# Spike encoding on Trainium2: x in four loads with a semaphore each, and the four lines of a step interleaved in memory

## The reference

```python
rates = relu(x) * 0.001
def step(voltage, rate_t):                 # 1024 steps; voltage starts at cond
    for _ in range(4):                     # four substeps
        voltage = voltage + rate_t
        spikes = floor(voltage)
        voltage = voltage - spikes
    return voltage, spikes                 # spikes of the last substep
h = all_spikes / 0.001
x = x + mixer(h, ...)                      # q, k, v projections, convolutions, delta rule, gates
x = x + experts(recurrence(cond, x), ...)  # gated recurrence, then top-1 of 8 experts
```

## Time and profile before

| | us |
|---|---|
| median of 3 runs | 1087.11 |
| lowest, highest | 1082.46, 1088.53 |
| profiled execution, its own time | 1088.54 |
| its span | 1086.6 |

### The profile page before, as it was taken

How to read it: one execution, slowest core, us unless ns; L and a number is a source line. 1 busy time by engine, 2 the same in 40 slices (tenths; PEclk the granted TensorE clock), 3 DMA queues, 4 the chain that set the end, 5 groups by cost and what they waited for, 6 DMA issues and landing times. The chain is left out here.

```text
span 1086.6 us, 13995 instructions
## 1 busy us (share of the span) xinstructions
PE 762.9 (70%) x5174; PEld 467.3 (43%) x5174; DVE 686.6 (63%) x967; ACT 496.0 (46%) x816; POOL 252.8 (23%) x227
## 2 busy tenths in 40 slices
PE   4720009979777055585865848999992779999995
PEld 1300003326657045574433414444441547667674
DVE  4999937872744999557579541999995413332331
ACT  5888735530433122365534414999993112222321
POOL 0000000000202000000050330799894023343331
PEclk9965559975778558898877869999996569999997
DMA  6700010000682000000200009100001911111100
GB/s 224 246 0 0 0 50 0 0 1 0 190 239 76 0 2 2 21 4 14 78 0 0 1 0 346 61 0 1 0 1 30 369 61 39 34 51 38 35 16 0
DMA packets 35509, 60.57 MB, mean 56 GB/s; under 512 B 8027, under 2 KB 22491, under 8 KB 34754
## 3 DMA queue, kind: packets, MB, share of 16 engines
q1 hardware_dynamic: 29826, 51.27, 14.6%
q0 software_dynamic: 3312, 6.31, 1.9%
q10 hardware_dynamic: 2304, 2.10, 0.6%
HBM read 55.20 MB, written 7.21 MB: 57 GB/s over the span
## 5 line engine op out<-in xcount | busy, mean ns | idle before, releaser
L1797 ACT ACTIVATE moe_ht<-x_tr,moe_b 128x128 f32<-128x128 f32 x184 | 49.9, 382 | 147.6 <-PE x_tr L1762 147.6
L1076 POOL TENSOR_TENSOR path<-path,mix_pr 128x1280 f32<-128x1280 f32 x16 | 38.3, 2424 | 247.7 <-DVE mix_pr L1238 247.7
L1753 PE MATMUL x_y<-moe_w,moe_ht 128*128 x368 | 85.0, 385 | 2.1 <-ACT moe_ht L1797 2.1
L1744 PE MATMUL x_hid<-w,moe_xt 128*128 x184 | 85.7, 610 | 0.9 <-DVE moe_xt L1887 0.7
L1753 PEld LDWEIGHTS x_y<-moe_w,moe_ht 128*128 128x128 f32 x368 | 69.4, 193 | 11.6 <-issue 2.8
L1894 DVE COPY moe_hid<-x_hid 128x512 f32<-128x512 f32 x46 | 31.9, 692 | 64.6 <-PE x_hid L1744 64.6
L205 PE MATMUL bad_sum<-spike_bad,ones 128*128 128x16 f32 x2 | 0.6, 386 | 88.5 <-ACT spike_outside L171 88.5
L1406 PE MATMUL r_bank<-recur_h_other,recur_wg 128*128 128x512 f32 x128 | 60.2, 592 | 0.0
L1402 PE MATMUL r_bank<-recur_zw,eye 128*128 128x512 f32 x112 | 57.2, 592 | 0.8 <-ACT recur_zw L1437 0.8
L201 PE MATMUL w_bank<-spike_wbuf,spike_pick 128*128 128x512 f32 x80 | 39.6, 655 | 21.2 <-DMA spike_wbuf<-in_gW 21.2
L367 PE MATMUL pj<-hs,proj_wqkv 128*128 128x512 f32 x96 | 46.4, 634 | 11.5 <-DMA mix_st<-in_c_spread 11.5
(11 more groups left out here) (274 smaller groups left out, 1878.2 us busy)
## 6 DMA issues: line engine op xcount, KB each, us to landing
spike_wbuf<-in_gW SPq DMA_DIRECT2D x8, 1280.0 KB, 6.2
w<-in_w1T SPq DMA_DIRECT2D x8, 1024.0 KB, 12.4
moe_w<-in_w2T SPq DMA_DIRECT2D x8, 1024.0 KB, 10.9
fir_band<-in_band_l SPq DMA_DIRECT2D x11, 512.0 KB
xT<-in_xT SPq DMA_DIRECT2D x4, 1024.0 KB, 6.0
fir_band<-in_band_m SPq DMA_DIRECT2D x11, 312.0 KB
mix_st<-in_band_l SPq DMA_DIRECT2D x5, 512.0 KB
z_rows<-recur_change SPq DMA_DIRECT2D x8, 256.0 KB, 3.8
```

The source lines that it names most:

```text
L1076: nc.gpsimd.tensor_tensor(x, x, w, ALU.mult).then_inc(s.weighted, 1)
L1744: last = nc.tensor.matmul(hid_bank[n][:], xt[:, c, :], m.w1[:, bass.ds(e, 1), c, n * N:(n + 1) * N].rearrange("p o n -> p (o n)"), start=( ...
L1753: last = nc.tensor.matmul(y_bank[:], ht[:, k, :], w2[:, bass.ds(e, 1), k, :].rearrange("p o n -> p (o n)"), start=(k == 0), stop=(k == K2 ...
L1797: nc.scalar.activation(ht[:, k, :], tr_bank[k // (K2 // 2)][:, k % (K2 // 2) * P:(k % (K2 // 2) + 1) * P], ACT.Relu, bias=b1[:, bass.ds(e, ...
```

## The change

Two edits in `load_and_spike`.

1. x comes in four loads of half a megabyte, one for each column group, each with a semaphore of its own. The two loads of the condition come first, with a semaphore `v_in`, and the pick matrix has `pick_in`. ScalarE's slope and VectorE's lines of the first four units wait for their own part; VectorE's first copy waits for the condition only, TensorE for the pick matrix. `done_with` has 27 semaphores instead of 22.
2. `line` is `[P, TU, SUB]`: the four substeps of a step lie side by side. First count reads it and writes `count` in order. The scan of L225 and the three L230 instructions now read and write `line` with a step of four float32 (16 bytes); they read their rates in order as before.

```diff
--- before.py
+++ after.py
@@ -68,7 +68,7 @@
         rate1 = [sb(f"rate1_{i}", [P, TU]) for i in range(2)]
         rate4 = [sb(f"rate4_{i}", [P, TU]) for i in range(2)]
         rate = [sb(f"rate{i}", [P, SU]) for i in range(RING)]
-        line = [sb(f"line{i}", [P, SUB, TU]) for i in range(2)]
+        line = [sb(f"line{i}", [P, TU, SUB]) for i in range(2)]
         volt = [sb(f"volt{i}", [P, SU]) for i in range(RING)]
         count = [sb(f"count{i}", [P, 2 + SU], I16) for i in range(RING)]
         over = [sb(f"over{i}", [P, 2 + SU], I16) for i in range(RING)]
@@ -88,14 +88,15 @@
         wbuf = sb("wbuf", [P, 2, W_CHUNK, HF])
         w_bank = own.enter_context(nc.psum_tensor("w_bank", [P, HF], F32))
         bad_sum = own.enter_context(nc.psum_tensor("bad_sum", [P, 2 * UNITS], F32))
-        (x_in, edge_set, w_used, started, rated, rated4, spread, summed, lined, rounded,
+        (v_in, pick_in, edge_set, w_used, started, rated, rated4, spread, summed, lined, rounded,
          counted, scanned2, flagged, recounted, corrected, scanned3, checked, spiked, joined,
          exact) = map(sem, (
-             "x_in", "edge_set", "w_used", "started", "rated", "rated4", "spread", "summed",
+             "v_in", "pick_in", "edge_set", "w_used", "started", "rated", "rated4", "spread", "summed",
              "lined", "rounded", "counted", "scanned2", "flagged", "recounted", "corrected", "scanned3", "checked",
              "spiked", "joined", "exact"))
         w_in = [sem(f"gate_w_in{i}") for i in range(2)]
-        m.done_with = [x_in, edge_set, w_used, started, rated, rated4, spread, summed, lined, rounded, counted, scanned2,
+        x_in = [sem(f"x_in{j}") for j in range(J)]
+        m.done_with = [*x_in, v_in, pick_in, edge_set, w_used, started, rated, rated4, spread, summed, lined, rounded, counted, scanned2,
                        flagged, recounted, corrected, scanned3, checked, spiked, joined, exact, *w_in]
 
         w_stat = d.gW1[D:, :].rearrange("(k p) n -> p k n", p=P)
@@ -106,9 +107,11 @@
         @block.sync
         def _(sp):
             for c in range(C):
-                sp.dma_start(m.xT[:, c * B:(c + 1) * B, :], d.xT[c * P:(c + 1) * P]).then_inc(x_in, 16)
-                sp.dma_start(v0[:, c * B:(c + 1) * B], d.condT[c * P:(c + 1) * P]).then_inc(x_in, 16)
-            sp.dma_start(pick[:], d.c_pick).then_inc(x_in, 16)
+                sp.dma_start(v0[:, c * B:(c + 1) * B], d.condT[c * P:(c + 1) * P]).then_inc(v_in, 16)
+            for j in range(J):
+                c, b = divmod(j, B)
+                sp.dma_start(m.xT[:, j, :], d.xT[c * P:(c + 1) * P, b]).then_inc(x_in[j], 16)
+            sp.dma_start(pick[:], d.c_pick).then_inc(pick_in, 16)
             for ch in range(CHUNKS):
                 if ch >= 2:
                     sp.wait_ge(w_used, ch - 1)
@@ -126,9 +129,10 @@
         @block.scalar
         def _(act):
             act.wait_ge(edge_set, 2 * RING + 3)
-            act.wait_ge(x_in, 5 * 16)
 
             def slope(u):
+                if u < J:
+                    act.wait_ge(x_in[u], 16)
                 if u >= 2:
                     act.wait_ge(summed, u - 1)
                 nc.scalar.activation(rate4[u % 2][:], x_of(u), ACT.Relu, scale=float(SUB * DT)).then_inc(rated4, 1)
@@ -146,7 +150,7 @@
                 act.wait_ge(lined, u + 1)
                 if u >= RING:
                     act.wait_ge(corrected, u - RING + 1)
-                nc.scalar.activation(count[i][:, 2:].rearrange("p (t s) -> p s t", s=SUB), line[u % 2][:], ACT.Relu,
+                nc.scalar.activation(count[i][:, 2:], line[u % 2][:].rearrange("p t s -> p (t s)"), ACT.Relu,
                                      bias=mid[:]).then_inc(rounded, 1)
 
             def flag(u):
@@ -191,7 +195,7 @@
 
         @block.tensor
         def _(pe):
-            pe.wait_ge(x_in, 5 * 16)
+            pe.wait_ge(pick_in, 16)
             for ch in range(CHUNKS):
                 pe.wait_ge(w_in[ch % 2], 16 * (ch // 2 + 1))
                 for i in range(W_CHUNK):
@@ -206,7 +210,7 @@
 
         @block.vector
         def _(dve):
-            dve.wait_ge(x_in, 5 * 16)
+            dve.wait_ge(v_in, C * 16)
             dve.wait_ge(edge_set, 2 * RING + 3)
             nc.vector.tensor_copy(v_start[:], v0[:]).then_inc(started, 1)
             dve.wait_ge(started, 1)
@@ -214,6 +218,8 @@
             def lines(u):
                 part, j = divmod(u, J)
                 i = u % 2
+                if u < J:
+                    dve.wait_ge(x_in[u], 16)
                 if u >= 2:
                     dve.wait_ge(spread, u - 1)
                 if part:
@@ -222,13 +228,13 @@
                 dve.wait_ge(rated4, u + 1)
                 if u >= 2:
                     dve.wait_ge(rounded, u - 1)
-                nc.vector.tensor_tensor_scan(line[i][:, SUB - 1, :], rate4[i][:], rate4[i][:], v_start[:, j:j + 1],
+                nc.vector.tensor_tensor_scan(line[i][:, :, SUB - 1], rate4[i][:], rate4[i][:], v_start[:, j:j + 1],
                                              ALU.add, ALU.bypass).then_inc(summed, 1)
                 dve.wait_ge(rated, u + 1)
                 dve.wait_ge(summed, u + 1)
                 for k in range(SUB - 1):
-                    last = nc.vector.scalar_tensor_tensor(line[i][:, k, :], rate1[i][:], float(k + 1 - SUB),
-                                                          line[i][:, SUB - 1, :], ALU.mult, ALU.add)
+                    last = nc.vector.scalar_tensor_tensor(line[i][:, :, k], rate1[i][:], float(k + 1 - SUB),
+                                                          line[i][:, :, SUB - 1], ALU.mult, ALU.add)
                 last.then_inc(lined, 1)
 
             def second_scan(u):
```

## The result

| | before | after |
|---|---|---|
| median of 19 runs each | 1085.47 us | 1090.85 us |
| lowest, highest | 1080.89, 1089.68 | 1085.54, 1093.46 |
| ratio, 95% interval | | 1.0049, 1.0033 to 1.0064 |
| span of the profiled execution | 1086.6 us | 1087.8 us |

The change makes the kernel 5.4 us slower. The forecast had the direction and about twice the size (+10.3 us).

A forecast was written before the change was run, and what follows sets the result against it. VectorE was taken to bound the spike stage. Start -4.3, first count -1.4, clears +0.3, lines +15.3, scans +0.4 summed to +10.3 us: 1097 us on a base of 1087.11, range 1083 to 1102.

The forecast's parts named there:

- VectorE sets the pace, and its gain or loss comes out one for one: Spike stage from 22.06 us to VectorE's last scan: VectorE alone sets the pace; its changes reach the stage's end fully.
- ScalarE's 23 us are worth only the first wait: First count in order: ScalarE 23 us less busy, but only VectorE's first wait for it counts, -1.4 us.
- Five clears, +0.3: SP clears five more semaphores ahead of the projection's loads, 0.06 us each: +0.3 us, all on the path.
- Part 0, -4.3: Start of the spike stage: first half megabyte of x lands at about 7.5 us instead of 11.75, -4.3 us.
- the late bound of 8.6: Part 0's landing in us if a half megabyte takes as long as the first whole megabyte (3.9 + 4.7).
- The lines, +15.3: 24 L230 instructions on VectorE, stepping 16 bytes, go from 688 to 1332 ns each: +15.3 us.
- I take the last: Price for VectorE's 16-byte step taken from ScalarE's L149, 2.29 ns an element, over VectorE's short and long rows.
- the middle rival: Lines priced by VectorE's long transpose rows: +8.2 us, sum +2.8, 1089.9 us; chance 0.27.
- The short rows: VectorE's short stepped instructions as price for the lines: 0.2 us as fixed cost, 4.0 us by the word.
- The scans, +0.4: Eight VectorE scans writing the line at a 16-byte step: +0.05 us each, +0.4 us in all.
- Read and write add up: Rival for the lines: a stepped read and a stepped write on VectorE add their costs, +25 us, 1112; chance 0.06.
- The page's 2.50: Skill page's ns a column for a destination stepping 24 words; L230 would grow 0.75 us, the sum be 14.

The follow-up runs named there:

- e7_x_first: Changed kernel with lines as two interleaved pairs, and part 0 of x issued ahead of the condition's two loads; one run, 1078.4 us.
- the probe: Kernel before plus a block ahead of the spike stage measuring VectorE and ScalarE instructions at various steps; run once for its trace, no kernel time given.

## Why the prediction was wrong

- **VectorE sets the pace, and its gain or loss comes out one for one**: right up to the stage's end, where -3.45 - 1.44 + 9.7 = +4.8 stand against +4.7 measured at the cast. With the 0.3 and 0.4 us behind it, and 0.2 more until the loads have landed, that is +5.6 at the first matmul, and +5.4 in the median.
- **ScalarE's 23 us are worth only the first wait**: right. 8 x 2.9 us went, 1.44 us of it counted, and its idle time ahead of the check grew.
- **Five clears, +0.3**: right, 0.28. Another 0.37 us at the barrier were not foreseen.
- **Part 0, -4.3**: -3.45. The landing was put at 7.5 and came at 8.4, near the late bound of 8.6. The terms ahead held: the first packets moved at 4.1, and the tiny loads had 1 us (1.05 in the sum). The term that failed is the 1.3 us for the half megabyte at 401 GB/s. At the 193 GB/s of 5 to 7 us and the 352 of the next half us, half a megabyte was through near 7.4, after 2.4 us, if the parts went in order. The tiny loads ahead are not the cause of that: in `e7_x_first`, with part 0 first, the first 0.52 MB moved from 3.5 to 6.0 us, at 207 GB/s.
- **The lines, +15.3**: +9.7, and this is the error. The failed step is "I take the last": of three kinds of rows I took ScalarE's int16 write because its step was nearest, and counted it among stores of single words, though it stores half words. The probe shows that this price goes with the type: at the same 8 bytes a float32 pays nearly nothing. VectorE's own long rows, the transposes at 1.70 ns a word, lay at 0.34 us for 512 words, and 0.41 was measured. The same engine and type far off in step were a better guide here than a near step on another engine and type. With 8.2 in its place the sum would have been +2.8, as the middle rival said; +5.4 lies between that and +10.3. With the measured 9.7, 3.45 and no cost for the scans it is +5.1. (At the chosen rate 24 x 0.644 is 15.5 us, not 15.3.)
- **The short rows**: they read too low, +6 and +10 ns for 31 words, where the probe's 32 words at step 4 cost 27. The argument that they were too short to show the price is not borne out: at step 4 an instruction of 32 words pays as much for a word as one of 512. The steps differ (32 words there), and why those rows show so little is open.
- **The scans, +0.4**: 0. 1283 ns against 1279; in order a scan takes longer than the 1060 ns of a stepped write alone.
- **Read and write add up**: no, 1.07 us for both at step 4 against 1.06 for either.
- **The page's 2.50** (the Trainium skill, "Vector Engine (DVE) Microarchitecture Reference", section "Measured stream behaviour on trn2") is right for a step of 24 words: 1440 ns, (1440 - 160) / 512 = 2.50. For 4 words, the step in question, the probe has 1.76. The page asks for adjacent words for the full rate; a step of two words, each in its own 8 bytes, ran at it too.
- **Range**: 1090.85 lies inside 1083 to 1102; the forecast of 1097 was 6 us off. Of these 1.6 are the base, since 1087.11 was the median of three runs and that of 19 is 1085.47; the forecast of the change, +10.3 against +5.4, was 4.9 off. Slower by over 0.5% was given 0.60 for a result at 0.49%, on the bound.

## What to carry to other kernels

When a layout is changed so that one engine runs in order, ask which engine now steps, and by how many words: the work moved here from one with room to the one without. Of prices that no row shows, trust the same engine and type before a near step; this case is one instance of it. In float32 a step of two words is free on VectorE and costs ScalarE 0.03 us for 512, so four interleaved streams can be kept as two pairs of two, and the reader takes pairs.

## What was not expected of the hardware

- The price of a step on VectorE is not monotone: 0, 0.14, 0.37, 0.37, 0.33, 0.75 and 0.34 us for 512 words at steps of 2, 3, 4, 6, 16, 24 and 32, the same for a read and a write, and once for both (0.44 for both at 32).
- ScalarE's int16 stores at 8 and 16 bytes take 1.34 and 2.46 us for 512, float32 ones 0.66 and 1.10.
- Two loads of 8 bytes for each partition keep the queue at 2 GB/s for 1 us. Issued on another queue beside half megabytes of x, they took 5.6 and 6.9 us to land, the second behind both parts issued by then.
